# A graph attention kernel on one core: moving three of sixteen multiplications by p to POOL, splitting two tiles' K times Q between DVE and ACT, and merging two small steps of the block's rescale

## The reference

```
q, k, v = layernorm(x) @ Wq + bq, @ Wk + bk, @ Wv + bv      # 8 heads of 64
logits[e, h] = sum_d q[row(e), h, d] * k[col(e), h, d] / 8 + edge_attr[e, h]
p = exp(logits - segment_max(logits)[row]);  att = p / segment_sum(p)[row]
y[n] = sum over the edges e of node n of att[e] * v[col(e)]
x = x + y @ Wo + bo;  x = x + ffn(layernorm(x))             # a small gated network
```

## Time and profile before

| | |
|---|---|
| time before, median of 3 runs | 3250.69 us (3249.51 to 3252.86) |
| the profiled execution: its time | 3252.61 us |
| the profiled execution: its span | 3250.8 us |
| busy in the span: PE, DVE, ACT, POOL | 2883.9, 2864.1, 2188.3, 2211.0 us |
| mean granted TensorE clock | 0.939 of full speed |
| edge loop, first and last gather issued | 1127.9 and 2868.4 us |

### The profile page before, as it was taken

How to read it: one execution, slowest core, us unless ns; L and a number is a source line. 1 busy time by engine, 2 the same in 40 slices (tenths; PEclk the granted TensorE clock), 3 DMA queues, 4 the chain that set the end, 5 groups by cost and what they waited for, 6 DMA issues and landing times.

```text
span 3250.8 us, 62874 instructions
## 1 busy us (share of the span) xinstructions
PE 2883.9 (89%) x11814; PEld 1680.8 (52%) x11939; DVE 2864.1 (88%) x20476; ACT 2188.3 (67%) x7706; POOL 2211.0 (68%) x2512
## 2 busy tenths in 40 slices
PE   4899888888888278999999999999999999989998
PEld 3555554445555135555555555555555555554444
DVE  8997777777777378999999999999999999998887
ACT  8332222222222048999999999999999999974444
POOL 0477777777777756777878778777878787851121
PEclk6798899888888689999999999999999999999999
DMA  6343333333333487888888888888888888841222
GB/s 188 84 136 105 107 111 107 113 107 107 106 104 93 163 307 251 262 262 259 259 261 263 260 259 265 259 264 259 264 260 260 260 263 259 259 140 61 83 79 71
DMA packets 259303, 615.95 MB, mean 189 GB/s; under 512 B 69771, under 2 KB 80343, under 8 KB 258658
## 3 DMA queue, kind: packets, MB, share of 16 engines
q0 software_dynamic: 144832, 443.72, 43.5%
q1 hardware_dynamic: 110434, 160.86, 16.5%
q10 hardware_dynamic: 3648, 7.34, 0.6%
HBM read 550.28 MB, written 61.49 MB: 188 GB/s over the span
## 4 chain that ended last, share of the span: by engine, by line
DVE 46%; POOL 23%; issue 14%; PE 12%; DMA 2%; DVEq 1%; ACT 1%; SPq 0%; POOLq 0%
DVE big L1339 25%; POOL rec_scratch L667 23%; DVE big L1449 12%; PE banks L2000 5%; PE banks L2065 2%; DVE big L1057 1%; DVEq L1449 1%; PE banks L1926 1%; PE banks L1979 1%; DMA big<-q_scratch 1%; DVE big L1434 1%; PE banks L1988 1%; DVE small L1401 1%; DMA big<-kv_scratch,small 1%; PE banks L2068 1%
## 5 line engine op out<-in xcount | busy, mean ns | idle before, releaser
L863 ACT ACTIVATE big<-big,small 128x65 f32<-128x65 f32 x6564 | 1605.1, 344 | 4.8
L688 POOL DMA_INDIRECT big<-kv_scratch,small x832 | 844.2, 1015 | 346.4 <-DVE big L1339 182.6
L1339 DVE SCALAR_TENSOR_TENSOR big<-banks,big 128x64 f32<-128x64 f32 x6656 | 1027.5, 213 | 32.6 <-DMA big<-kv_scratch,small 17.5
L667 POOL DMA_INDIRECT rec_scratch<-big,small x782 | 773.3, 989 | 323.4 <-issue 237.7
L1926 PE MATMUL banks<-big,small 128*128 x1664 | 889.7, 616 | 73.2 <-DVE big L1339 56.5
L1979 PE MATMUL banks<-big,small 128*128 128x260 f32 x3328 | 882.2, 388 | 45.6 <-POOL small L696 21.4
L1979 PEld LDWEIGHTS banks<-big,small 128*128 128x128 f32 x3328 | 615.0, 190 | 452.9 <-issue 271.9
L1817 PE MATMUL banks<-big 128*128 128x512 f32 (+1 forms) x1176 | 604.1, 662 | 34.8 <-DVE big L1047 34.8
L1449 DVE SCALAR_TENSOR_TENSOR big<-big,loS,banks 128x520 f32 x832 | 618.6, 744 | 6.3 <-PE banks L1979 4.2
L696 POOL TENSOR_SCALAR small<-iotaF,small 128x128 f32<-128x128 f32 x832 | 527.2, 634 | 60.5 <-PE banks L1979 34.8
L1339 DVE DVE_READ_ACCUMULATOR big<-banks,big 128x1 f32 x6656 | 513.5, 77 | 0.1
(11 more groups left out here) (273 smaller groups left out, 2639.7 us busy)
## 6 DMA issues: line engine op xcount, KB each, us to landing
rowR<-lo_rows SPq DMA_DIRECT2D x97, 256.0 KB
big<-src_rows SPq DMA_DIRECT2D x97, 256.0 KB, 3.6
big<-in_x_dram SPq DMA_DIRECT2D x96, 256.0 KB, 4.0
big<-kv_scratch,small POOLq DMA_INDIRECT x832, 5.3
rec_scratch<-big,small POOLq DMA_INDIRECT x782
kv_scratch<-big SPq DMA_DIRECT2D x48, 260.0 KB
q_scratch<-big SPq DMA_DIRECT2D x48, 256.0 KB
kv_scratch<-big SPq DMA_DIRECT2D x48, 256.0 KB
```

The source lines that it names most:

```text
L667: e.indirect_dma_start(recd, bass.IndirectOffsetOnAxis(ap=ridx[:, c % 4, j:j + 1], axis=0), rec[:, 8 * c + j, :], None).then_inc(s_sc[c % ...
L688: e.indirect_dma_start(KV[:, vat(t):vat(t) + YW + D], None, KVd, bass.IndirectOffsetOnAxis(ap=recB[b_ % 4][:, t % 16, 9:10].bitcast(i32), ...
L863: ins = e.activation(heads(Vr(t), h, h + 1), heads(Vr(t), h, h + 1), ACT.Copy, scale=ph[:, h:h + 1])
L1339: ins = e.scalar_tensor_tensor(k_, QB[t % 2][:, 64 * h:64 * h + 64], 1.0, k_, ALU.mult, ALU.mult, accum_out=Lr[t // 16 % 2][:, t % 16, h:h ...
```

## The change

Four edits, all in the edge loop:

- Tiles with t % 16 in (3, 8, 13), t < 809 (152 of them): `pva` on ACT is left out; POOL does the whole V row in one TENSOR_TENSOR of 128x520 (`pvp`) in its step t + 21, behind `gather` and `one_hot`. It waits for the block's `s_ex` (p). ACT's `p_exp`, PE's `yt` wait for `s_pvp` too.
- Tiles with t % 16 in (4, 10), t < 793 (99 of them): DVE makes one product of 128x512 in place of K in the first half of `kq` and raises `s_rd`; nothing in the second half. ACT's `sums(t)`, at the head of its step t + 2, sums each head's 64 columns by 8 ACTIVATE with an accumulator output, and raises `s_sum`. The gather that overwrites this K, and `lb`, wait for `s_sum` too.
- `scale_parts`: one SCALAR_TENSOR_TENSOR of 8x128 (one-hot times factor) in place of a compare of 8x128 and an 8x8 step; ACT takes 1 off the factor (`p_less`) behind `p_fac`, and PE multiplies by the identity.
- The constant `nI` is gone.

```diff
+        summed = [t % 16 in (4, 10) and t < LAST - 16 for t in range(T)]
+        on_pool = [t % 16 in (3, 8, 13) and t < LAST for t in range(T)]
...
# POOL
                 q.wait_ge(s_rd, k + 1)
+                if k >= 0:
+                    q.wait_ge(s_sum, sum_base + sum_at[k])
...
+            def pvp(t):
+                v = Vr(t).rearrange("p (h d) -> p h d", d=65)
+                q.wait_ge(s_kv[t % 8], 16 * (t // 8 + 1))
+                q.wait_ge(s_ex, t // 16 + 1)
+                e.tensor_tensor(v, v, pB[t // 16 % 2][:, t % 16, :].rearrange("p (h a) -> p h a", a=1).broadcast_to([128, 8, 65]), ALU.mult).then_inc(s_pvp, 1)
...
                 if s - DEL - 2 >= 0:
                     one_hot(s - DEL - 2)
+                if 0 <= s - DEL + 2 < T and on_pool[s - DEL + 2]:
+                    pvp(s - DEL + 2)
...
# ACT
+            def p_less(b_):
+                q.wait_ge(s_fac, 2 * b_ + 1)
+                e.activation(fac[0:8, 0:1], fac[0:8, 0:1], ACT.Copy, bias=-1.0).then_inc(s_fac, 1)
+
+            def sums(t):
+                q.wait_ge(s_rd, t + 1)
+                q.wait_ge(s_x2, t // 16 - 1)
+                for h in range(8):
+                    k_ = Kr(t)[:, 64 * h:64 * h + 64]
+                    ins = e.activation(k_, k_, ACT.Copy, accum_out=Lr[t // 16 % 2][:, t % 16, h:h + 1])
+                ins.then_inc(s_sum, 1)
...
-                if s >= DEL:
+                if 2 <= s < T + 2 and summed[s - 2]:
+                    sums(s - 2)
+                if s >= DEL and not on_pool[s - DEL]:
                     pva(s - DEL)
                 if r_ == 5 and 0 <= b_ < NB:
                     p_fac(b_)
+                    p_less(b_)
                 if r_ == 6 and 0 <= b_ < NB:
                     p_exp(b_)
...
# DVE
+                if summed[t]:
+                    if not half:
+                        e.tensor_tensor(Kr(t), QB[t % 2], Kr(t), ALU.mult).then_inc(s_rd, 1)
+                    return
...
-                e.tensor_tensor(Aoh[0:8, :], iotaF[0:8, :], llb[0:8, max(b_ - 1, 0):max(b_ - 1, 0) + 1].broadcast_to([8, 128]), ALU.is_equal).then_inc(s_bd, 1)
-                e.scalar_tensor_tensor(Bd[0:8, :], ident[0:8, 0:8], fac[0:8, 0:1], nI[0:8, :], ALU.mult, ALU.add).then_inc(s_bd, 1)
+                e.scalar_tensor_tensor(Aoh[0:8, :], iotaF[0:8, :], llb[0:8, max(b_ - 1, 0):max(b_ - 1, 0) + 1], fac[0:8, 0:1].broadcast_to([8, 128]),
+                                       ALU.is_equal, ALU.mult).then_inc(s_bd, 1)
...
# PE
-                q.wait_ge(s_pva, t + 1)
+                q.wait_ge(s_pva, t + 1 - pvp_at[t])
+                if pvp_at[t]:
+                    q.wait_ge(s_pvp, pvp_base + pvp_at[t])
```

More of the change, by code:

```diff
@@ L319, in build @@
         HV = 4
+        summed = [t % 16 in (4, 10) and t < LAST - 16 for t in range(T)]
+        sum_at = [sum(summed[:t + 1]) for t in range(T)]
+        s_sum, sum_base = s_ab, 2 * NCH
+        on_pool = [t % 16 in (3, 8, 13) and t < LAST for t in range(T)]
+        pvp_at = [sum(on_pool[:t + 1]) for t in range(T)]
+        s_pvp, pvp_base = s_hist, NCH
         def vat(t):
@@ L845, in p_exp @@
                 q.wait_ge(s_dt, b_ + 1)
-                q.wait_ge(s_pva, 16 * (b_ - 1))
+                if b_ >= 2:
+                    q.wait_ge(s_pva, 16 * (b_ - 1) - pvp_at[16 * (b_ - 1) - 1])
+                    q.wait_ge(s_pvp, pvp_base + pvp_at[16 * (b_ - 1) - 1])
                 e.activation(flat(pB[b_ % 2]), DP, ACT.Exp).then_inc(s_ex, 1)
@@ L851, in p_fac @@
                 q.wait_ge(s_dd, b_ + 1)
-                q.wait_ge(s_bd, 2 * b_)
+                q.wait_ge(s_bd, b_)
                 e.activation(fac[0:8, 0:1], fac[0:8, 1:2], ACT.Exp, scale=-1.0).then_inc(s_fac, 1)
+            def p_less(b_):
[8 more added lines that the diff above has]
+                ins.then_inc(s_sum, 1)
             def heads(v, h0, h1_):
@@ L1269, in _ @@
             e.tensor_copy(GT[0:8, :].rearrange("p (t h) -> p t h", h=8), ident[0:8, 0:8].rearrange("p (a h) -> p a h", a=1).broadcast_to([8, 16, 8])).then_inc(s_const, 1)
-            e.tensor_scalar(nI[0:8, :], ident[0:8, 0:8], -1.0, None, ALU.mult).then_inc(s_const, 1)
             for k in range(2):
@@ L1346, in lb @@
                 q.wait_ge(s_rd, 16 * b_ + 16)
+                q.wait_ge(s_sum, sum_base + sum_at[16 * b_ + 15])
                 e.tensor_tensor(Lr[b_ % 2], Lr[b_ % 2], recB[b_ % 4][:, :, 0:8], ALU.add).then_inc(s_lb, 1)
@@ L1388, in growth @@
                 q.wait_ge(s_cf, 2 * b_ + 2)
-                q.wait_ge(s_fac, b_)
+                q.wait_ge(s_fac, 2 * b_)
                 e.scalar_tensor_tensor(fac[0:8, 1:2], c[0:8, 0:1], c[0:8, 17:18], c[0:8, 17:18], ALU.max, ALU.subtract).then_inc(s_dd, 1)
@@ L1414, in scale_parts @@
             def scale_parts(b_):
-                q.wait_ge(s_fac, b_ + 1)
+                q.wait_ge(s_fac, 2 * b_ + 2)
                 q.wait_ge(s_s1, b_)
-                e.tensor_tensor(Aoh[0:8, :], iotaF[0:8, :], llb[0:8, max(b_ - 1, 0):max(b_ - 1, 0) + 1].broadcast_to([8, 128]), ALU.is_equal).then_inc(s_bd, 1)
-                e.scalar_tensor_tensor(Bd[0:8, :], ident[0:8, 0:8], fac[0:8, 0:1], nI[0:8, :], ALU.mult, ALU.add).then_inc(s_bd, 1)
+                e.scalar_tensor_tensor(Aoh[0:8, :], iotaF[0:8, :], llb[0:8, max(b_ - 1, 0):max(b_ - 1, 0) + 1], fac[0:8, 0:1].broadcast_to([8, 128]),
+                                       ALU.is_equal, ALU.mult).then_inc(s_bd, 1)
             def pv(t):
@@ L1517, in f_x1 @@
                 e.tensor_tensor(xx[0:n, :], xx[0:n, :], BK[1 + k][0:n, :], ALU.add).then_inc(s_x1, 1)
-            q.wait_ge(s_const, 10)
+            q.wait_ge(s_const, 9)
             for s in range(T + DEL + 4):
@@ L1579, in _ @@
             q.wait_ge(s_yt, T)
-            q.wait_ge(s_pva, T)
+            q.wait_ge(s_pva, T - pvp_at[T - 1])
             e.memset(FT, 0.0).then_inc(s_ftz, 1)
@@ L1964, in scale1 @@
             def scale1(b_):
-                q.wait_ge(s_bd, 2 * b_ + 2)
+                q.wait_ge(s_bd, b_ + 1)
                 q.wait_ge(s_ex, b_ + 1)
                 q.wait_ge(s_sca, b_ - 1)
-                e.matmul(S1, Aoh[0:8, :], Bd[0:8, :], start=True, stop=True).then_inc(s_s1, 1)
+                e.matmul(S1, Aoh[0:8, :], ident[0:8, 0:8], start=True, stop=True).then_inc(s_s1, 1)
             def yt(t):
-                q.wait_ge(s_pva, t + 1)
+                q.wait_ge(s_pva, t + 1 - pvp_at[t])
                 q.wait_ge(s_pvv, t - LAST + 1)
+                if pvp_at[t]:
+                    q.wait_ge(s_pvp, pvp_base + pvp_at[t])
                 q.wait_ge(s_oh2, t + 1)
```

## The result

The changed kernel takes 3463.22 us (median of 4 runs, 3460.04 to 3463.62) against 3250.28 us for the kernel before, a ratio of 1.0654 (1.064 to 1.0667): 213 us slower, where 130 had been forecast. The range ended at 3445. The direction was right, and so was the place; the size was not.

A forecast was written before the change was run, and what follows sets the result against it. The prediction took DVE and ACT as both full, ACT tightest. A loop over p of 35.8 us against 33.1 added 2.7 us in each of 48 blocks, 130 us on 3252.6: 3380 us as the median, range 3255 to 3445.

The forecast's parts named there:

- What bounded the kernel: In the edge loop, DVE and ACT both busy 99.7% or more, ACT the tightest: 30.7 of 33.1 us in heads.
- POOL's reserve of 3.5 us: POOL's 16 gather steps take 29.6 of a block's 33.1 us, leaving 3.5 us, not the 6.6 of "80% busy".
- The wait on p: POOL's first product waits for p_exp, closing a loop of 35.8 us against 33.1, 2.7 us a block; chance 0.64.
- step 2: On ACT, sums(B+4) start at 3.25 us, ahead of p_exp, and take 8 x 0.32 = 2.56, to 5.81.
- the blocking that I gave no term: POOL and DVE instructions with two SBUF inputs lock each other out; up to 1.27 us each, left out of the sum.
- step 6: The loop's end: gather(B+19) lands 5.3 us after its issue at 30.5, and kq of that tile starts at 35.8.
- the dear rival: Everything at the dear end: accumulator read 0.24 us, longest product, a loop of 38.2 us, 3495 us in all; chance 0.10.
- The wait for the sums: gather(t + 5) waits for ACT's sums of tile t: no cost while POOL is late, otherwise up to 2.5 us each.

The follow-up runs named there:

- e3: The changed kernel without the sums on ACT and without the products on POOL, only the merged rescale step: 3259.03 us, ratio 1.003 to the kernel before.
- e10: The changed kernel with POOL's products at t % 16 = 5, 7, 9 and sums for 13 alone: 3252.46 us, ratio 1.0007 to the kernel before.
- e9: The changed kernel with POOL's products at t % 16 = 5, 7 and sums for 13 alone: 3232.96 against 3251.55 us for the kernel before, ratio 0.9942.
- e1: The changed kernel without the sums on ACT, keeping POOL's three products and the merged rescale: 3367.72 us, ratio 1.0363 to the kernel before.
- e5: The changed kernel with p_exp ahead of the sums of tile 4 in ACT's order: 3673.01 against 3499.68 us for the kernel before, ratio 1.0484.
- e7: The changed kernel without sums, POOL's products at t % 16 = 5, 7, 9: 3501.49 against 3499.68 us for the kernel before, ratio 1.0006.
- e6: The changed kernel with POOL's product of tile 13 one POOL step earlier: 3675.59 against 3499.68 us for the kernel before, ratio 1.0498.
- e4: The changed kernel with POOL's products at t % 16 = 7, 11, 15 instead of 3, 8, 13: 3405.39 us, ratio 1.0477 to the kernel before.
- e8: The changed kernel with POOL's products at t % 16 = 5, 9 and sums for 10 alone: 3535.51 against 3499.68 us for the kernel before, ratio 1.0114.
- e11: The changed kernel with p_exp ahead of tile 4's sums and POOL's product of tile 13 one step earlier: 3392.28 us, ratio 1.043 to the kernel before.

## Why the prediction was right in direction and wrong in size

**What bounded the kernel, and POOL's reserve of 3.5 us: right.** e3 came out as the forecast for ACT as the tightest engine said. The reserve is shown by e10 against e9: two products fit and three use up what DVE had gained.

**The wait on p: right.** The forecast ahead of e1, worked out from the measured 8.85, was met to 2 us, e5 shows the block following p, and e7 shows that products whose p is ready are free. e7's tiles keep clear of `lb` too, so e1 and e7 alone don't part the wait on p from the blocked `lb`; e6 puts a price on the second.

**The step that failed first is step 2**, "ACT stands at `sums(B+4)`". It doesn't. ACT can run ahead of PE only to the next `one_hot_T`, which it meets in step B+4. There PE's `rows_oh` stands behind `cx`, which waits for DVE's `carries` at the head of step B+3, and behind `yt`. So ACT is let go 2.04 us after the start of `kq(B+3)`. From there come 0.49 for L841, 1.92 for a tile, 0.33 for `p_fac` and `p_less`: 4.78 instead of 3.25. I had looked at where ACT waits for DVE and not at where it meets PE; in the kernel before, this wait hardly shows (L824 waited 15.0 us for PE's `rows_oh`, in 4 cases, against 267.7 us in 112 in the changed kernel). It added 1.53 us, of which the cheaper sums gave back 0.65.

**The second is the blocking that I gave no term, and with it step 6.** In the sum below it is the larger of the two. The row of the dear rival named `lb`, `back1` and `spread` as what POOL could lock out, and left it at a possibility; step 6 then let the loop end at the landing of `gather(B+19)`. That landing came as forecast (35.76), but it was not what `kq(B+19)` waited for. The product of t % 16 = 13 overlapped `lb` in 44 of 52 blocks, and each time `lb` ended 0.16 us behind it. "SBUF — State Buffer" of the Trainium skill, section "SBUF: two separate sides", says just this of a DVE instruction with two SBUF inputs. For POOL's product the trace agrees: `lb` went from 283 to 1150 ns in the median. Instructions with one input in PSUM kept their length beside the products: heads of `kq` took 214 ns in the mean beside one and 215 elsewhere, `ya` 748 and 746. For POOL's one-hot, which reads SBUF as well, it doesn't agree: in the kernel before, 44 of the 52 `lb` overlapped one and took 283 ns in the median, at most 421. Had I put down that POOL's step B+18 and DVE's step B fall together in the steady state, the term could have been worked out.

Together, by the way that the block takes: the first product starts at 9.00 instead of 7.98 (+1.02), the three products and the steps between take 21.57 instead of 22.35 (-0.78), and `lb` and DVE's steps behind it take 0.16 + 6.66 = 6.82 from the last product's end, where the forecast's way over the gather and its landing takes 5.47 (+1.35). 35.8 + 1.6 = 37.4. Over 48 blocks the 1.6 to 1.7 us are the 80 us that were missing. e6 gave back less than 1.35 because a third way, over `kq(B+15)`, is only 0.75 shorter.

**Terms that were off the other way.** POOL's product takes 1.06 us, not 1.27. A sum of 64 columns with its read takes 0.24 us, not 0.32. Both made the time shorter, so without them the forecast would have been further off.

**The wait for the sums: right for this kernel, wrong as a rule.** While POOL is late for p it is covered. As soon as p comes sooner or the products move to where it is ready, it costs: it is one of the two waits that left e4 with 58 instead of over 150 us back, it took part of e5's gain, and e8 is slower than before.

**Not settled.** Of the 213 us, e11 gives back 72 and e1 95 on its own; no run took away the sums and the blocked `lb` at once with the tiles in place, so the price of the wait for p alone isn't measured. Of the same 43 blocks of the changed kernel, 7 took over 38 us. In five of them `kq(B+15)` started only at 29.3 to 31.8 and `lb` behind it ended over 1 us after the product; in the other two POOL took 0.9 and 1.3 us more from the first product to the last. Why those were late I haven't found. Why a gather starts 0.75 us behind ACT's last sum (in e4, e5, e8 and e9 alike), and 0.28 us behind DVE's `kq` before, wasn't tried.

## What to carry to other kernels

Work that is moved to an idle engine brings its inputs along: POOL had 3.5 us a block to spare, but by running ahead, and an operand that is ready late turned its lead into the chain that set the block. So choose by step, not by busy time: without the sums, three products cost 118 us at tiles 3, 8, 13, where they wait for p and hold up `lb`, and nothing at 5, 7, 9. Before moving work to POOL, list DVE's instructions with two SBUF inputs and the steps in which they run; and for each hand-over to ACT count what stands in its order between the last point where it must wait anyway and the new instruction.

## What the runs showed of the hardware

- ACT's accumulator read is its own instruction, but not an extra cost here: the ACTIVATE with an accumulator output is followed after 0.14 us by the read, and the next starts 0.09 us later, 0.24 us a head, as for one without a sum.
- POOL's product of 128x520 with one broadcast input took 1.047 to 1.071 us in the loop of the changed kernel, less than L703's 1.27 for 128x512 in the earlier trace rows.
- A DVE instruction with two inputs in SBUF that meets POOL's product ends a fixed time after it: `lb` 0.16 us behind it in 44 of 44 cases, up to 1.56 us long instead of 0.28, and the scan `back1` 0.29 us behind it in 41 of 41 in e4, 1.73 us in the median instead of 0.41. That holds also for an `lb` that started up to 0.34 us ahead of the product. POOL's one-hot alone does not do it (44 `lb` of the kernel before, at most 0.42 us), and the scan `fwd1` (L1394), which has one input in PSUM, kept its 0.42 us beside three products in e4.
- A gather that waited for ACT's last accumulator read started 0.7 to 0.8 us after its end (79 cases in e4, 39 in e8, 40 in e9); the one at 2061.37 in the earlier trace rows, which waited for DVE's accumulator read, started about 0.28 us after that.
